# 34 of 1024 softmax score tiles taken from ScalarE's ring and exponentiated on VectorE by a polynomial

## The reference, cut to what matters

```python
q, k, v = proj(Wq) * mod, proj(Wk) * mod, proj(Wv) * mod      # (1, 16, 2048, 8)
scores = einsum('bhid,bhjd->bhij', q, k) / sqrt(8) * cos(2*pi*(i - j)/S)
w = softmax(scores, axis=-1)
w = (w + roll(w, 1, axis=-1)) / sqrt(2)
attn = einsum('bhij,bhjd->bhid', w, v) ... @ Wo
# experts: top 2 of 8 by small logits, silu(x @ w1a) * (x @ w1g) @ w2, weighted sum
out = x + attn + experts
```

## Time and profile before

| what | us |
|---|---|
| median of 3 runs | 595.48 |
| lowest and highest run | 593.88, 599.56 |
| the profiled execution | 593.97 |
| its span in the profile | 592.2 |
| PE busy in the span | 543.2 |
| ScalarE busy | 520.6 |
| VectorE busy | 223.6 |

### The profile page before, as it was taken

The page is one execution under the profiler, slowest core; times in us unless marked ns, Lnnn a source line. Parts: engine busy times, 40 slices in busy tenths (PEclk is TensorE's granted clock), DMA queues, the critical chain, the costliest instruction groups (busy, mean ns, idle before and its releaser), DMA issues.

```text
span 592.2 us, 19062 instructions
## 1 busy us (share of the span) xinstructions
PE 543.2 (92%) x7948; PEld 255.3 (43%) x7948; DVE 223.6 (38%) x517; ACT 520.6 (88%) x480; POOL 97.3 (16%) x102
## 2 busy tenths in 40 slices
PE   2867998887999999999999999999999999999884
PEld 1342333332444444444445445444544545454333
DVE  7976346500413434344343434334343212221134
ACT  2648989997899999999999999999999999999991
POOL 5210068543001010010101010010101001010000
PEclk9987999999899999999999999999999999999999
DMA  7852035214644232241423233232323313200402
GB/s 220 175 170 94 1 104 145 87 33 126 144 132 128 62 103 78 78 112 48 131 53 96 85 94 96 85 95 66 98 71 95 95 44 94 54 11 7 147 2 74
DMA packets 60890, 53.76 MB, mean 91 GB/s; under 512 B 33244, under 2 KB 50294, under 8 KB 60546
## 3 DMA queue, kind: packets, MB, share of 16 engines
q1 hardware_dynamic: 58082, 47.48, 30.2%
q0 software_dynamic: 2272, 4.72, 2.2%
q10 hardware_dynamic: 448, 0.30, 0.2%
HBM read 38.68 MB, written 13.78 MB: 89 GB/s over the span
## 4 chain that ended last, share of the span: by engine, by line
PE 67%; ACT 13%; issue 11%; DVE 4%; DMA 3%; SPq 1%; POOL 0%; ACTq 0%; DVEq 0%
PE ps L1374 33%; PE ps L1348 21%; ACT big L697 11%; PE ps L1281 7%; PE ps L1291 4%; DMA qk_parts<-store 1%; DVE attnT L761 1%; PE ps L1183 1%; DMA acc<-in_L_attn_x 1%; PE ps L1318 1%; ACT store L654 1%; SPq L452 1%; DMA store<-in_L_ffn_w 1%; DVE big L786 0%; DMA slots_x<-attnT,slot 0%
## 5 line engine op out<-in xcount | busy, mean ns | idle before, releaser
L697 ACT ACTIVATE big<-ps 128x1536 f32<-128x1536 f32 (+1 forms) x410 | 481.4, 1236 | 28.8 <-PE ps L1348 24.7
L1374 PE MATMUL ps<-big,vh 128*32 128x256 f32 (+1 forms) x3968 | 265.7, 394 | 0.0
L1348 PE MATMUL ps<-qa,ka 49*128 49x512 f16 x896 | 166.0, 388 | 19.7 <-ACT big L697 12.9
L1374 PEld LDWEIGHTS ps<-big,vh 128*32 128x32 f32 x3968 | 108.6, 110 | 113.9 <-issue 65.5
L1348 PEld LDWEIGHTS ps<-qa,ka 49*128 49x128 f16 x896 | 37.5, 94 | 139.2 <-ACT big L697 107.5
L593 POOL DMA_INDIRECT results<-y,row_of x39 | 37.9, 971 | 270.8 <-DVE y L984 269.4
L1281 PE MATMUL ps<-xgT,store 128*32 128x128 f32 x1716 | 66.5, 276 | 2.8 <-DMA store<-in_L_ffn_w 2.8
L1281 PEld LDWEIGHTS ps<-xgT,store 128*32 128x32 f32 x1716 | 55.0, 112 | 18.4 <-issue 6.0
L969 DVE SCALAR_TENSOR_TENSOR cs<-cs,ps 128x384 f32<-128x384 f32 x39 | 21.6, 554 | 91.9 <-ACT cs L689 91.9
L1047 DVE TENSOR_REDUCE m<-ps 128x1 f32<-128x512 f32 x64 | 44.1, 689 | 31.2 <-PE ps L1385 31.2
L984 DVE TENSOR_SCALAR y<-ps,weight_of 128x128 f32<-128x128 f32 x39 | 13.7, 351 | 98.2 <-PE ps L1291 98.2
(11 more groups left out here) (186 smaller groups left out, 201.9 us busy)
## 6 DMA issues: line engine op xcount, KB each, us to landing
store<-in_L_ffn_w SPq DMA_DIRECT2D x39, 352.0 KB, 3.1
store<-in_L_ffn_w SPq DMA_DIRECT2D x39, 192.0 KB, 3.4
qk_parts<-store SPq DMA_DIRECT2D x8, 512.0 KB, 4.1
qa<-qk_parts SPq DMA_DIRECT2D x27, 128.0 KB
slots_x<-vh SPq DMA_DIRECT2D x8, 330.0 KB, 7.6
cs<-slots_x SPq DMA_DIRECT2D x80, 32.0 KB, 2.7
store<-results SPq DMA_DIRECT2D x4, 512.0 KB, 5.6
ka<-qk_parts SPq DMA_DIRECT2D x31, 64.0 KB, 2.4
```

The lines of the kernel that those rows point to most:

```text
L697: nc.scalar.activation(probs[:, prob_of(tiles[0]):prob_of(tiles[-1]) + 1, :], ps[:, bank_of(tiles[0]):bank_of(tiles[-1]) + 1, :], ACT.Exp, ...
L1348: ins = nc.tensor.matmul(ps[:, bank_of(n), :], k[at:at + KQ, P * o:P * o + P], q[at:at + KQ, CW * c:CW * c + CW], start=True, stop=True, t ...
L1374: ins = nc.tensor.matmul(ps[32 * c:32 * c + 32, O_BANKS[p % 2], cols], vh[:, p % 2, o + 8 * b, :], probs[:, prob_of(n), cols], start=k == ...
```

## The change

ScalarE exponentiates 990 tiles in 198 rounds; the last 2 tiles of heads 2 to 11 and of head 15, and the last 4 of heads 12 to 14, 34 in all, go aside:

- PE multiplies such a tile in a round of its head from the second quad on, where a job's matmul would stand, beside the third score tile, at the other row position and into the idle sum bank (`aside_scores`). Jobs wait until the head's asides are out.
- VectorE takes it from PSUM into SBUF with a scale and a lower bound (`take_aside`, 512 columns). Of each pair of tiles (1024 columns) it then computes 2 to the power y: the whole part by adding a large constant and shifting bits, the fractional part by a degree-five polynomial (`power_chunk`). That is eight instructions in six chunks, one chunk a round in heads with two such tiles, two chunks a round in heads 12 to 14. The chunks stand in a round ahead of the expert's part.
- The product is taken by the last quad of the head from `aside_probs`, after a wait for the pair. The polynomial is left unnormalised, and ScalarE's exponential gets the same factor by a bias, `lift`.
- The ring's tiles of a head are 64, 62 or 60, and the value pieces of a head are spread evenly over them (`even_halves`).
- The 39 expert tiles are spread over 148 rounds instead of 156: a tile starts after 4 or, eight times, 3 rounds (`tile_round`).

```diff
+ASIDE_OF = (0,) * 2 + (2,) * 10 + (4,) * 3 + (2,)
+RING_OF = tuple(PER_HEAD - n for n in ASIDE_OF)
+SCORE_TILES = RING_FIRST[H]
+ASIDE_QUAD = 1
+CHUNKS = 6
-ROUNDS_A_TILE = 4
+EXPERT_ROUNDS = 148
...
+        def even_halves(n):
+            p = head_of(n)
+            return QUADS * HALVES * p + QUADS * HALVES * (n - RING_FIRST[p]) // RING_OF[p]
...
+        def tile_round(m):
+            return EXPERTS_AT + -(-EXPERT_ROUNDS * m // TILES)
...
         def rounds():
+                chunks = chunks_left[0:ASIDE_OF[p] // 2]
+                del chunks_left[0:len(chunks)]
+                if w % QUADS >= ASIDE_QUAD and scored < ASIDE_FIRST[p + 1] and aside_tile(p, scored - ASIDE_FIRST[p])[2] == half:
+                    aside = (p, scored - ASIDE_FIRST[p])
+                    scored += 1
+                    if scored % 2 == 0:
+                        chunks_left += [(scored // 2 - 1, k) for k in range(CHUNKS)]
-                even = (RING * HALVES * r - NC) // NC
+                    pieces = range(done, max(min(ready, even_halves(exps - 2)), done))
...
-                                     ACT.Exp, scale=ISQ8 / (OPERAND * OPERAND)).then_inc(exp_done, 1)
+                                     ACT.Exp, bias=lift[:], scale=SCALE).then_inc(exp_done, 1)
...
+            def take_aside(p, i):
+                n = ASIDE_FIRST[p] + i
+                dve.wait_ge(aside_scored, n + 1)
+                nc.vector.tensor_scalar(reduced[n // 2 % 2][:, CW * (n % 2):CW * (n % 2) + CW], ps[:, O_BANKS[(p - 1) % 2], :],
+                                        SCALE / float(np.log(2.0)), LEAST_POWER, ALU.mult, ALU.max).then_inc(aside_taken, 1)
+            def power_chunk(n, chunk):
+                y = reduced[n % 2]
+                if chunk == 0:
+                    then(nc.vector.tensor_scalar(whole_power, y, MOST_POWER, TO_WHOLE, ALU.min, ALU.add))
+                    then(nc.vector.scalar_tensor_tensor(y, whole_power, TO_WHOLE, y, ALU.subtract, ALU.subtract))
+                elif chunk == 1:
+                    then(nc.vector.tensor_scalar(power_bits, power_bits, 23, None, ALU.logical_shift_left))
+                    then(nc.vector.scalar_tensor_tensor(poly, y, POWER[0], y, ALU.add, ALU.mult))
+                elif chunk < CHUNKS - 1:
+                    then(nc.vector.scalar_tensor_tensor(poly, poly, POWER[chunk - 1], y, ALU.add, ALU.mult))
+                else:
+                    nc.vector.scalar_tensor_tensor(aside_probs[...], poly, POWER[CHUNKS - 2], whole_power,
+                                                   ALU.add, ALU.mult).then_inc(aside_ready, 1)
...
+                for n, chunk in chunks:
+                    power_chunk(n, chunk)
                 if step == 0:
                     if m < TILES:
                         rows_out(m)
...
+                    if k == QUADS - 1:
+                        after(pe, aside_ready, ASIDE_FIRST[p + 1] // 2)
```

More of the change, by code:

```diff
@@ L62 @@
 PER_HEAD = NT * NC
-SCORE_TILES = H * PER_HEAD
 QUADS = PER_HEAD // NC
+ASIDE_OF = (0,) * 2 + (2,) * 10 + (4,) * 3 + (2,)
+RING_OF = tuple(PER_HEAD - n for n in ASIDE_OF)
+RING_FIRST = tuple(sum(RING_OF[:p]) for p in range(H + 1))
+ASIDE_FIRST = tuple(sum(ASIDE_OF[:p]) for p in range(H + 1))
+SCORE_TILES = RING_FIRST[H]
+ASIDE_QUAD = 1
+CHUNKS = 6
 HALVES = 2
@@ L217, in build @@
         second = sb("second", [P, 2, S], F32)
+        reduced = [second[:, 0, 2 * CW * i:2 * CW * i + 2 * CW] for i in range(2)]
+        whole_power, poly = (second[:, 1, 2 * CW * i:2 * CW * i + 2 * CW] for i in range(2))
+        power_bits = whole_power.bitcast(mybir.dt.int32)
+        aside_probs = sb("aside_probs", [P, 4, CW], F32)
+        lift = sb("lift", [P, 1], F32)
         rotated = whole_rotated[0:2] + [second[:, i, :] for i in range(2)]
@@ L309, in prob_of, with head_of, block_of, quad_of @@
             return n % PROBS
-        def tile_at(n):
[L313 to L319, removed]
+        def head_of(n):
+            return sum(n >= first for first in RING_FIRST[1:H])
+        def block_of(r):
+            s = r % 8
+            return r // 8, s if s < NC else s - NC ^ 1, r % 2
+        def tile_at(n):
+            p = head_of(n)
+            return p, *block_of(n - RING_FIRST[p])
+        def quad_of(n):
+            p = head_of(n)
+            return p * QUADS + (n - RING_FIRST[p]) // NC
+        def tiles_before_quad_ends(w):
+            p, k = w // QUADS, w % QUADS
+            return RING_FIRST[p] + min(NC * k + NC, RING_OF[p])
+        def even_halves(n):
+            p = head_of(n)
+            return QUADS * HALVES * p + QUADS * HALVES * (n - RING_FIRST[p]) // RING_OF[p]
+        def aside_tile(p, i):
+            return block_of(RING_OF[p] + i)
         def groups_for(n):
@@ L367, in rounds @@
                     j += 1
-                ready = min(RING * r, SCORE_TILES) // NC * HALVES
-                even = (RING * HALVES * r - NC) // NC
-                pieces = range(done, max(ready if r == ROUNDS else min(ready, even), done))
+                pieces = range(done, done)
+                if r == ROUNDS:
+                    pieces = range(done, H * QUADS * HALVES)
+                elif r > 0:
+                    exps = RING * r
+                    ready = quad_of(exps) * HALVES
+                    pieces = range(done, max(min(ready, even_halves(exps - 2)), done))
                 done = pieces.stop
-                yield r, jobs, pieces
+                yield r, jobs, pieces, aside, chunks
         def quads_in(pieces):
@@ L610, in scatter_rows @@
                                              xn_placed[:, t, :], None).then_inc(scattered, 16)
-            result_at = {RING * result_round(m) // NC + 1: m for m in range(TILES)}
+            result_at = {(even_halves(RING * result_round(m)) + 2) // HALVES: m for m in range(TILES)}
             for w in range(SCATTER_AT, H * QUADS):
@@ L1054, in make_exact_shift @@
                                         ALU.mult, ALU.add).then_inc(exact_shift_ready, 1)
-            for r, jobs, pieces in rounds():
+            def take_aside(p, i):
[6 more added lines that the diff above has]
+                if chunk == 0:
+                    dve.wait_ge(aside_taken, 2 * n + 2)
+                    after(dve, aside_ready, n)
+                    then(nc.vector.tensor_scalar(whole_power, y, MOST_POWER, TO_WHOLE, ALU.min, ALU.add))
[6 more added lines that the diff above has]
+                else:
+                    p = sum(2 * n >= first for first in ASIDE_FIRST[1:H])
+                    at = 2 * n - ASIDE_FIRST[p]
+                    dve.wait_ge(pv_done, QUADS * p * HALVES)
+                    nc.vector.scalar_tensor_tensor(aside_probs[:, at:at + 2, :].rearrange("p a n -> p (a n)"), poly, POWER[CHUNKS - 2], whole_power,
+                                                   ALU.add, ALU.mult).then_inc(aside_ready, 1)
+            for r, jobs, pieces, aside, chunks in rounds():
                 m, step = expert_step(r)
@@ L1383, in max_job @@
                 after(pe, m_reduced, j)
+                after(pe, aside_taken, ASIDE_FIRST[p + 1])
                 at = 64 * c
@@ L1401, in _ @@
             pe.wait_ge(v_ready, 4)
-            for r, jobs, pieces in rounds():
+            for r, jobs, pieces, aside, _ in rounds():
                 for job in jobs[:-1]:
```

62 lines of the change are left out of this document (42 added, 20 removed).

## The result

| | before | after |
|---|---|---|
| median of the runs on the same chip, us | 594.93 (593.88 to 599.56) | 616.42 (615.48 to 618.00) |
| runs | 4 | 4 |
| profiled execution and its span | 593.97, 592.2 | 615.48, 613.6 |

The ratio is 1.0354, 95% interval 1.0316 to 1.0392: the changed kernel is slower by 3.5%, 21.1 us. The forecast was slower by 12.0, 607.5 us. The sign was foreseen and the time lies within the range, but 9 us of it have no term in the sum.

What follows compares the result with a forecast made beforehand. The prediction took the kernel to be ScalarE-bound, with a little of PE in it. Its terms, -16.3 + 0 + 12.7 + 1.5 + 14.1 = +12.0 us, gave 607.5 us on the median, range 588 to 618.

Steps and rivals of the forecast that it cites:

- A: Exponentials removed from ScalarE, 205 rounds becoming 198 at 2.40 us each: -16.3 us.
- The bias of the exponential I cost at nothing: ScalarE's exponentials: a per-partition bias adds no time; were it 10 ns each, 396 of them make +4 us.
- C: Alignment of value pieces and expert steps on PE, results and second widenings behind more pieces: +12.7 us, bounds +5 and +17.
- D: Work added to VectorE: +1.5 us in heads 2 to 11 and 15, +14.1 in heads 12 to 14.
- 2.40 us a round: ScalarE's two partly overlapped exponentials with the hand-over, taken as its own need in every round.
- B: 34 matmuls on PE beside the third score: 0 us, or 7.5 if each took a slot of its own.
- The wait near 0.7: Sign in heads 3 to 11: ScalarE idles near 0.7 us for scores when a result stands behind three pieces, not 0.27.
- the walk: Round-by-round count in head 12 of VectorE's chunks delaying PE's widenings: 4.7 us, three times that for heads 12 to 14.
- 1: Rival: ScalarE's saving shows in full since PE and VectorE have slack; 579 us, or 584; chance 13%.
- 2: Rival: VectorE's chunks hide everywhere and only the alignment is paid; 592 us; chance 20%.
- 4: Rival: VectorE's tensor_scalar of 1024 columns takes 1.22 us, 18 us more work; 620 us; chance 5%.
- 3: Rival: longer PE waits in heads 12 to 14 drop its clock to half pace; 616 us; chance 9%.

Runs made afterwards that it cites:

- e2: The kernel before, with a bias of zero from a column in SBUF in its exponentials, nothing else: 613.65 us, ratio 1.0345.
- e1: The changed kernel without the exponential's bias, the factor taken out of the polynomial's argument instead: 602.56 us, ratio 1.0175 to before.
- e5: The changed kernel without the bias and without the polynomial, the 34 takes kept: 591.38 us, ratio 0.9968 to before.
- e8: e7 with the number of value pieces in a round following the expert step: 586.14 us, ratio 0.9874 to before.
- e12: The changed kernel as it is, run again on the same chip: 618.76 us, ratio 1.0410 to before.
- e4: The kernel before with every expert step one round later, nothing else changed: 611.95 us, ratio 1.0326.
- e7: The changed kernel without bias, 28 tiles aside (two in each of heads 2 to 15), expert tiles over 156 rounds: 590.88 us, ratio 0.9977 to before.
- e10: e8 with the eight additions of the experts' results moved from VectorE to GpSimd: 584.40 us, ratio 0.9855 to before.

## Why the prediction was right or wrong

- **A, the exponentials.** The count held, the price didn't. The step that failed is the sentence "The bias of the exponential I cost at nothing", with "+4" for 10 ns each: it measures 91 ns each, and 10.6 us in this kernel (20.4 in before, e2), within some 2 to 3. I had called it a per-partition number in an instruction of a microsecond or more, without a row for it; the trace of before had no exponential with a bias from SBUF, and so the bound should have been a wide one. As an edit that touches every round, it was the one to bound with most care. It is as large as the whole miss: 12.0 + 10.6 = 22.6, against 21.1. That the other terms add up so closely is partly luck, since C came out larger than its value and D, with the bias in, smaller.
- **What bounds a round.** The prediction reads 2.40 us a round as ScalarE's own need. By the starts above ScalarE alone wants 2.25; nearly every large exponential of before waited for its scores, in the free rounds too, which the prediction says never hold it up. The price of a removed round, 2.40, isn't harmed by that, since a round as a whole goes; but it is why 0.18 a round of longer exponentials costs only about 0.1.
- Why 10.6 here and 20.4 in before: where PE or VectorE makes the round late anyway, ScalarE's extra time is hidden. By the table, heads 3 to 11 pay 8.4 (0.08 a round). Heads 12 to 14 show nothing, but e1 has its clock drop there, some 3 us, so they pay about one. The first 43 rounds show 5.3, but those rounds differ by 2.9 between e1 and e5 too.
- **B, the matmuls beside the third score.** Not shown. B alone wasn't run, and it is in e5's 16.8 us together with C. For a value near nothing speaks e8, which keeps 28 of these matmuls: its rounds 43 to 187 take 375.2 us (281.8 and 93.4) against 372.6 in before. The wait of 2.10 in e12 shows that an aside can hold PE up, in some executions.
- **C, alignment.** +12.7 forecast; +14.4 by e5's ratio with A taken at its 16.3, and 16.8 by the stretches of e5, at the upper bound of 17. The wait near 0.7 is in the rows. e4 shows the mechanism with nothing else changed, e8 against e7 gets 6.1 back.
- **D, VectorE.** The prices of the instructions were right. In heads 12 to 14 it is 14.0 without the bias against 14.1 forecast, but the match is partly luck: some 2.7 of it are the clock drop, which the walk didn't have. In the changed kernel itself it is 9.4. That the longer rounds give VectorE more room there is likely and wasn't tested. The +1.5 for the other heads wasn't there: 0.0, and 0.7 with the bias.
- **The rivals.** 1 and 2 fell: C and D are both paid. 4 fell by VectorE's groups. 3 was right as a contribution in some executions, once in e1 and twice in e12, and wrong as the outcome.
- **The sum split by runs:** A, B and C -1.9 (e5), D +12.3 (e1 against e5), bias +10.6 (after against e1). These are three steps on one way from before to the changed kernel, so they add up to its 21 us by construction; that they do checks nothing. What can be compared is each step with its forecast: -3.6, +15.6, 0.

## What to carry to other kernels

An operand added to an instruction that runs in every round is a change of the inner loop: price it from a row that has it, or measure it alone, before anything else in the diff. Work of two periods in one queue (here pieces 2, 3 and steps in fours) is worth as much by its alignment as by its amount: one shifted by one round cost 19 us, which was more than seven rounds of ScalarE. A round's length isn't the need of the engine that looks busy throughout: compare the distance of its starts with the shortest one in the trace. Spare time on an engine counts only between two steps that others wait for, so keep a piece of extra work shorter than that gap.

## What the runs showed of the hardware

- A bias read from a column in SBUF makes an exponential on ScalarE 91 ns longer, at 1024 and at 1536 columns alike. The Trainium skill (ScalarE: Activation LUTs, What ACT_TABLE_LOAD costs) says that each operand of one number a partition, passed by pointer, adds about 93 ns to an ACTIVATE; the rows agree. From that figure, an estimate of 0.093 for each of 396 exponentials is 37 us: it would have named the missing term ahead of the run, and overstated it, since only 10.6 showed in the time.
- After waits of PE of 2.75 and 2.74 us at the same place of the same kernel, the granted clock stayed at 1.00 in one execution and fell to 0.50 for about 6 us in the other. After 2.95 in e1 it fell. In heads 12 to 14 of these three, waits of 1.9 and less left it alone, while 2.10 in head 3 of e12 was followed by 0.51.
- The kernel before shows the clock's part too. Of its 19 executions beside e5, the eight with a mean granted clock of 0.975 took 593.59 to 596.12 us, the others, with 0.983 to 0.986, 589.68 to 593.46.
- While GpSimd ran additions of 128x512 in e10, a tensor_tensor of 128x128 on VectorE took 1.03 us instead of 0.29 and a tensor_scalar of 128x256 1.35 instead of 0.28. Work moved to an idle GpSimd can slow VectorE beside it.
- On VectorE, an fp32 scalar_tensor_tensor of 1024 columns takes 1217 to 1225 ns, a tensor_scalar of as many 686, and an int32 shift 688.
